# Copying a transposed k tile out of PSUM once, and letting the DMA queue place its low and high parts

## The reference

```
h = layernorm(x) * (1 + ca) + sa
q, k, v = h @ Wq, h @ Wkv            # 16 heads, 4 + 4 heads of 64
q, k = rotate(q), rotate(k)          # q*cos + rotate_half(q)*sin
attn = softmax(q @ k.T / 8)          # 4 query heads share a k and a v
x = x + ga * ((attn @ v) @ Wo + bo)
h = layernorm(x) * (1 + cb) + sb
x = x + gb * (gelu(h @ bw1.T + b1) @ bw2.T + b2)
```

## Time and profile before

| | |
|---|---|
| median of three runs | 766.95 us |
| the profiled execution's own time | 766.3 us |
| its span, first to last instruction | 764.5 us |
| mean granted TensorE clock | 0.962 |
| busy: PE / DVE / ACT / POOL | 89% / 79% / 77% / 71% |
| DMA: bytes moved, share of the 16 engines' time on the kernel's queue | 24.4 MB, 14.7% |

### The profile page before, as it was taken

The page is one execution under the profiler, slowest core; times in us unless marked ns, Lnnn a source line. Parts: engine busy times, 40 slices in busy tenths (PEclk is TensorE's granted clock), DMA queues, the critical chain, the costliest instruction groups (busy, mean ns, idle before and its releaser), DMA issues.

```text
span 764.5 us, 14217 instructions
## 1 busy us (share of the span) xinstructions
PE 677.3 (89%) x3829; PEld 541.3 (71%) x3829; DVE 607.1 (79%) x1275; ACT 592.2 (77%) x1213; POOL 539.4 (71%) x459
## 2 busy tenths in 40 slices
PE   3588999999999999999999999999999999866665
PEld 3465787868777778777777777777778787655654
DVE  6767878787878787888878787878787878549995
ACT  2578988888888888888889888888888888626664
POOL 1568787868696969696877878687878786505564
PEclk9599999999999999999999999999999999978888
DMA  8011111110101111111111101111111111000001
GB/s 234 14 29 30 30 31 30 31 28 18 40 16 28 29 29 29 29 29 29 29 29 29 26 19 29 29 29 29 29 30 30 30 30 30 16 1 17 25 27 42
DMA packets 31578, 24.72 MB, mean 32 GB/s; under 512 B 16688, under 2 KB 26944, under 8 KB 31552
## 3 DMA queue, kind: packets, MB, share of 16 engines
q1 hardware_dynamic: 31552, 24.40, 14.7%
HBM read 4.47 MB, written 2.10 MB: 9 GB/s over the span
## 4 chain that ended last, share of the span: by engine, by line
PE 44%; DVE 21%; issue 18%; ACT 8%; POOL 5%; DMA 1%; DVEq 1%; SPq 0%; POOLq 0%; ACTq 0%
PE o_ps L977 10%; PE unit_ps L934 8%; DVE w_all L728 4%; DVE o_t L733 4%; PE score_ps L952 4%; PE score_ps L954 4%; PE unit_ps L907 4%; PE unit_ps L918 4%; POOL probs_lo L483 3%; DVE recip_hi L748 2%; DVE rot_a L718 2%; DVE rot_b L720 1%; PE unit_ps L928 1%; POOL rot_sum L468 1%; PE unit_ps L891 1%
## 5 line engine op out<-in xcount | busy, mean ns | idle before, releaser
L483 POOL TENSOR_TENSOR probs_lo<-probs,probs_hi 128x512 fp32r<-128x512 f32 x208 | 270.8, 1314 | 51.9 <-ACT probs_hi L622 50.6
L468 POOL TENSOR_TENSOR rot_sum<-rot_a,rot_b 128x512 f32<-128x512 f32 (+1 forms) x96 | 113.2, 1179 | 109.2 <-DVE rot_b L720 108.9
L728 DVE TENSOR_REDUCE w_all<-unit_ps 128x2 f32<-128x512 f32 x256 | 166.4, 683 | 7.9 <-PE unit_ps L918 6.7
L620 ACT ACTIVATE probs<-score_ps 128x512 f32<-128x512 f32 x256 | 150.9, 589 | 3.5 <-PE score_ps L954 3.2
L622 ACT ACTIVATE probs_hi<-score_ps 128x512 fp32r<-128x512 f32 x256 | 152.2, 594 | 0.0
L918 PEld LDWEIGHTS unit_ps<-k_hi,q_hilo 128*128 128x128 f32 x512 | 95.1, 193 | 37.9 <-DVE o_t L733 6.0
L907 PEld LDWEIGHTS unit_ps<-ident_r,qk_rot 128*128 128x128 f32 x640 | 95.7, 194 | 29.4 <-DVE o_t L733 13.3
L733 DVE TENSOR_TENSOR o_t<-o_un,unit_ps 64x256 f32<-64x256 f32 x256 | 106.8, 417 | 8.5 <-PE unit_ps L928 3.8
L952 PE MATMUL score_ps<-q_hilo,k_hi 128*128 128x512 f32 x256 | 108.1, 422 | 2.9 <-DMA q_him<-neg_max_t 1.5
L472 POOL TENSOR_TENSOR qk_rot<-rot_sum,qk_rot 128x512 fp32r<-128x512 f32 (+1 forms) x96 | 105.6, 1106 | 5.2 <-ACT qk_rot L570 5.2
L918 PE MATMUL unit_ps<-k_hi,q_hilo 128*128 128x256 f32 x512 | 106.1, 291 | 2.7 <-DVE rot_b L720 1.4
(11 more groups left out here) (110 smaller groups left out, 1206.4 us busy)
## 6 DMA issues: line engine op xcount, KB each, us to landing
q_him<-q_hilo SPq DMA_DIRECT2D x64, 256.0 KB
out_x<-w_all SPq DMA_DIRECT2D x16, 128.0 KB, 1.8
xa<-in_L_attn_x SPq DMA_DIRECT2D x3, 640.0 KB, 6.9
q_him<-neg_max_t SPq DMA_DIRECT2D x64, 4.0 KB
w_all<-in_L_attn_Wq SPq DMA_DIRECT2D x1, 512.0 KB, 4.2
w_sb<-in_L_ffn_w SPq DMA_DIRECT2D x2, 256.0 KB, 3.1
wo_sb<-in_L_attn_Wo SPq DMA_DIRECT2D x1, 512.0 KB, 7.5
sums<-o_un SPq DMA_DIRECT2D x32, 8.0 KB, 2.0
```

The costliest lines, as they stand in the source:

```text
L468: pool.tensor_tensor(total, rot_a[k % 2][:, 0:heads, :], rot_b[k % 2][:, 0:heads, :], ALU.add).then_inc(rot_summed, 1)
L483: pool.tensor_tensor(probs_lo[s % 2][:, jc, :, :], probs[s % 2][:, jc, :, :], probs_hi[s % 2][:, jc, :, :].bitcast(F32), ALU.subtract).the ...
L620: act.activation(probs[s % 2][:, jc, :, :].rearrange("p h i -> p (h i)"), score_ps[jc][:, :], ACT.Exp, scale=SCALE)
L728: dve.tensor_reduce(neg_max[u[1] // 4][:, first:first + C], ps[:, :].rearrange("p (c j) -> p c j", c=C), AX.X, ALU.max, negate=True).then_ ...
```

## The change

ACT copies the transposed tile of k once, all 128 partitions, to `k_hi2` (high in 0 to 63, low in 64 to 127). Then SP issues two DMAs of 128 KB for each of the two k tiles of a batch: `k_low_part` moves the low part from partitions 64 to 127 of `k_hi2` to `k_lo1`, and when that has landed `k_high_part_again` writes the high part over it. PE's bank wait and its two data waits go to the new semaphores. SP's written order takes the four new issues in among the old ones.

```diff
+            def k_low_part(st, half, batch):
+                sp.wait_ge(kt_ready, st.count(2, half + 1, batch))
+                sp.dma_start(k_lo1[st.par(batch)][0:DH, 2 * half:2 * half + 2, :].bitcast(F32),
+                             k_hi2[st.par(batch)][DH:P, 2 * half:2 * half + 2, :].bitcast(F32)).then_inc(k_lo_in[half], 16)
+            def k_high_part_again(st, half, batch):
+                sp.wait_ge(k_lo_in[half], st.count(16, 16, batch))
+                sp.dma_start(k_hi2[st.par(batch)][DH:P, 2 * half:2 * half + 2, :].bitcast(F32),
+                             k_hi2[st.par(batch)][0:DH, 2 * half:2 * half + 2, :].bitcast(F32)).then_inc(k_hi_in[half], 16)
             def step(st):
...
                     maxima(st, 2, 0)
                     high_parts(st, 3, 0)
+                if st.prep:
+                    k_low_part(st, 0, 1)
+                if st.attn:
                     maxima(st, 3, 0)
+                if st.prep:
+                    k_high_part_again(st, 0, 1)
+                if st.attn:
                     gather_sums(st, 0, 0)
+                if st.prep:
+                    k_low_part(st, 1, 1)
+                if st.attn:
                     spread_reciprocals(st, 0, 0)
+                if st.prep:
+                    k_high_part_again(st, 1, 1)
                 if st.prep:
                     high_parts(st, 0, 1)
                     maxima(st, 0, 1)
...
                 if kind == "kt":
-                    high = ps[0:DH, :].rearrange("p (g i) -> p g i", g=2)
-                    for half in range(2):
-                        act.activation(k_hi2[par][half * DH:half * DH + DH, 2 * u[1]:2 * u[1] + 2, :], high,
-                                       ACT.Copy).then_inc(k_hi_ready, 1)
-                    act.activation(k_lo1[par][0:DH, 2 * u[1]:2 * u[1] + 2, :],
-                                   ps[DH:P, :].rearrange("p (g i) -> p g i", g=2), ACT.Copy).then_inc(k_lo_ready, 1)
+                    act.activation(k_hi2[par][:, 2 * u[1]:2 * u[1] + 2, :],
+                                   ps[:, :].rearrange("p (g i) -> p g i", g=2), ACT.Copy).then_inc(kt_ready, 1)
...
                 if kind == "kt":
-                    pe.wait_ge(k_lo_ready, st.count(2, u[1] + 1, of))
+                    pe.wait_ge(kt_ready, st.count(2, u[1] + 1, of))
...
                     if h % 8 == 0:
-                        pe.wait_ge(k_hi_ready, st.count(4, h // 4 + 2, ahead(u)))
+                        pe.wait_ge(k_hi_in[h // 8], st.count(16, 16, ahead(u)))
...
                 if s % 4 == 0 and jc == 0:
-                    pe.wait_ge(k_lo_ready, st.count(2, s // 4 + 1))
+                    pe.wait_ge(k_lo_in[s // 4], st.count(16, 16))
```

More of the change, by code:

```diff
@@ L341, in adaln_layer @@
             sem("v_hi_ready"), sem("rot_parts"), sem("rot_summed"), sem("rot_high"), sem("rot_ready"))
-        k_hi_ready, k_lo_ready, q_ready = sem("k_hi_ready"), sem("k_lo_ready"), sem("q_ready")
+        kt_ready, q_ready = sem("kt_ready"), sem("q_ready")
+        k_lo_in, k_hi_in = [sem(f"k_lo_in{i}") for i in range(2)], [sem(f"k_hi_in{i}") for i in range(2)]
         q_him_in = [sem(f"q_him_in{i}") for i in range(4)]
```

## The result

The changed kernel takes 777.13 us (median of 4 runs, 775.72 to 777.74), the kernel before, on the same chip, 767.17 us (766.94 to 769.63). The ratio is 1.012, with 95% from 1.0099 to 1.0142: slower by 1.2%; the two medians differ by 9.96 us. The forecast was 773.5 us, with 771 to 776.5 as the case's own range. The profiled execution took 775.72 us with a span of 773.9 us, 9.4 more than before.

A forecast was written before the change was run, and what follows sets the result against it. PE and DVE, handing work to each other in slots 5 to 7, were taken as the bound. 14 steps x 0.48 = 6.7 us on 766.3 gives 773.0, plus 0.65 for the median 773.6; predicted 773.5 us, range 771 to 776.5.

The forecast's parts named there:

- the case's own range: Whole kernel: 771 to 776.5 us around the forecast of 773.5 us, which had chance 0.64.
- the wide range: Whole kernel: 763.6 to 777.5 us, taking in the forecast, the cancelling and most of the hidden case.
- ACT's copies: ACT's k copies: 1.35 us less per tile, 43 us of ACT time, mostly off the path.
- the stop at `s 0`: PE, slot 5: a wait of about 0.25 us per step goes, at most 3.75 us gained over 15 steps.
- The transfers: The four new k DMAs per prepared batch: hidden ahead of their readers, costed at nothing.
- The upper bound of the delay: Gathering of the sums: 8 KB stand behind the 128 KB, 0.6 us more, 1.2 us late at most.
- The delay of the gathering: SP, between maxima and gathering of the sums: one inserted issue plus a wait delays the gathering by 0.6 us.
- The rival of a hidden delay: DVE, slot 5: small instructions escape POOL, PE's gain remains, 763.5 us; decided by gathering before 343.9; chance 0.19.
- The collision: DVE, slot 5: late cast is shut out until POOL's `probs_lo` ends at 347.77; `rot_a` comes 1.09 us late.
- the 0.48 us per step: DVE's next `rot_a`, steps 1 to 14: 0.48 us late (0.3 to 0.65), 6.7 us in all.
- The stretch of 5.08 us: DVE from one `rot_a` to the next without waiting, read from step 0: 5.08 us.
- The 0.15: DVE, slot 5: `rot_a` starts 0.15 us after POOL's end, as read from step 0.

The follow-up runs named there:

- e1: Changed kernel with SP's issue of the high part again (half 0) moved ahead of the maxima of quarter 3: 764.90 us, ratio 0.9972 to the kernel before.
- e6: Changed kernel with ACT's single copy of k but none of the four k DMAs or their waits: 767.85 us, ratio 0.999 to the kernel before.
- e4: Changed kernel with one more DMA issue between the high part again and the gathering: 779.02 us, ratio 1.0148 to the kernel before.
- e2: Changed kernel with the high part again (half 0) issued behind the gathering: 772.79 us, ratio 1.0052 to the kernel before.
- e5: Kernel before with one unused DMA issue added between the maxima of quarter 3 and the gathering: 778.55 us, ratio 1.0143 to the kernel before.
- e8: Changed kernel with only recip_hi computed by RECIPROCAL from the sums, recip_lo still a subtraction: 772.36 us, one run.
- e10: Repeat of e2, gathering issued first in the changed kernel, on the chip of e9: 769.91 us, ratio 1.0026 to the kernel before.
- e9: Repeat of e1, high part issued before the maxima in the changed kernel, on another chip: 765.97 us, ratio 0.9976 to the kernel before.
- e3: Changed kernel with recip_hi and recip_lo also computed by RECIPROCAL from the sums, the split left out: 768.76 us, ratio 1.001 to the kernel before.

## Why the prediction was right

The direction, the place and the mechanism were right; the size was not. Forecast were 6.55 us more than before, 9.96 were measured. 777.13 us lies above the 771 to 776.5 of the case's own range, and inside the wide range by 0.4 us only. That range takes in a gain as well, and its upper end of 777.5 isn't worked out from any term, so that it holds the result is luck.

**ACT's copies.** The place was right: the stop at `s 0` goes, DVE takes over, and a new stop shows at the transposed maxima. ACT's busy time fell by 33 us, not by the 38 or the 43 that the prediction names. Where the gathering isn't late, the gain is 0.2 to 0.25 us per step (e1, e6), as worked out.

**The transfers.** Costed at nothing, and e6 beside e1 leaves 0.1 us for two steps. The upper bound of the delay (another 0.6 us for the 128 KB on the way) was not met: the landing stays at 2.0 us.

**The delay of the gathering.** 0.6 us forecast, 0.62 measured. The issue itself took 0.47 us, less than the least of 0.495 that the prediction gave for SP: that was one line's least, and the same profile has issues of 0.37 us (L435). That the result doesn't depend on it once it is past the margin is what e4 shows. The rival of a hidden delay was to decide at a gathering issued before 343.9, or +3.62 in the step: e1 and e2 (+3.37, +3.36) are on its side and lose nothing, after, e5 and e4 (+3.98, +3.94, +4.61) are on the other and lose 0.6 to 0.67 us. No run stands between +3.37 and +3.94, so the point itself isn't measured. The rival was one issue away, and e1 is it, at 764.9 us, where it was put at 763.5.

**The collision.** Its place, the instruction, POOL's partner and the step in which DVE has no slack left were right. The term that was mis-sized is the 0.48 us per step: it measured 0.67, just outside the ends given (0.3 to 0.65). The stretch of 5.08 us was right (5.10). The start of it was not: POOL started at +6.27 instead of +6.20, and `rot_a` came 0.25 us behind POOL's end instead of 0.15. Together that is 0.17 of the missing 0.19, and the stretch has the rest. The prediction had POOL's instruction where it was; in the steps shown it starts at +6.27 or +6.28 in the kernels with the four transfers (after, e1 to e4, e8), and at +6.20 to +6.22 without them (before, e5, e6). So the transfers, costed at nothing, have a small part in it. The 0.15 was read from step 0, where `rot_a` follows the subtraction after 0.09 us; here it follows after 0.19 (352.37 to 352.56). Why, stays open. With 0.67 the same sum gives 14 x 0.67 = 9.4 us. The 14 steps measured 9.0, as one of them lost 0.35 only, and the other 0.4 us of the spans stand ahead of step 1, where the prediction saw no loss. A single execution doesn't tell whether that 0.4 is the change's.

**What stays open.** Why e2 and e10, whose profiled steps are clean, have medians 4 to 8 us above those of e1 and e9: step 0, the stretches at half clock and the end can each move an execution by 1.5 us or more, but no profile of a slower execution of e2 is there to show it. And why only a few steps have such a stretch, when PE makes the same stop for `o_t` in steps that have none (0.65 us). The runs here don't tell.

## What to carry to other kernels

A DMA that is free in itself still takes its issue, here half a microsecond, of a queue that works in order, so look at what is queued behind it and who stands waiting for that; put the issue where the queue is idle. The slack of a late instruction is not only the time to its next reader: here it was the 0.37 us to the start of another engine's instruction that shuts it out. Past that point the late instruction ends with that other one, and being later still cost no more (e4). When an engine's share of the chain jumps while its busy time doesn't, look whether it blocks others; here it did.

## What the runs showed of the hardware

- RECIPROCAL on 128x16 runs beside POOL's TENSOR_TENSOR at its usual 0.25 to 0.26 us (e3), where CAST takes 1.25 us (after) and the subtraction 0.98 us (e8) for 0.17.
- A shut-out DVE instruction can lose to several POOL instructions in a row: 5.56 us for two `xn` (e6), which take 0.58 with POOL idle (before, at 6.84) and 1.57 where one instruction of POOL meets them (before, at 348.04).
- A transfer of 8 KB issued 0.59 us behind one of 128 KB lands in the same 2.0 us as without it (after beside before).
